# Scores of two graphs in every second slot, score banks doubled, adjacency and values in one bank, two late outputs off VectorE

## What is computed

```python
# per graph; rows are nodes (128), columns features (512)
h = maximum(layernorm(x), 0)
A = adj @ h                                        # layer 0: both weights are adj
x = x + max over columns of maximum(A + b0, 0)     # one number per row
h = maximum(layernorm(x), 0)                       # layer 1
q, k, v = h @ Wq + bq, h @ Wk + bk, h @ Wv + bv
w = softmax(q @ k.T / 8 + (-1e9 where adj == 0))   # per head, over k's nodes
x = x + w @ v
```

## Time and profile before

| | |
|---|---|
| median of three runs | 1332.76 us |
| profiled execution, its own time | 1333.84 us |
| its span, first to last instruction | 1331.8 us |
| TensorE's mean granted clock | 0.993 of full |
| busy share: TensorE, GpSimd, VectorE, ScalarE | 98%, 83%, 81%, 71% |
| longest of the chain that ended last | TensorE, 92% |

### The profile page before, as it was taken

The page is one execution under the profiler, slowest core; times in us unless marked ns, Lnnn a source line. Parts: engine busy times, 40 slices in busy tenths (PEclk is TensorE's granted clock), DMA queues, the critical chain, the costliest instruction groups (busy, mean ns, idle before and its releaser), DMA issues.

```text
span 1331.8 us, 30435 instructions
## 1 busy us (share of the span) xinstructions
PE 1299.0 (98%) x11177; PEld 682.6 (51%) x11177; DVE 1075.3 (81%) x2236; ACT 942.4 (71%) x1423; POOL 1108.3 (83%) x1161
## 2 busy tenths in 40 slices
PE   6999999999999999999999999999999999999994
PEld 3455555555555555555555555555555555555552
DVE  7688887888888888888788788788788878878677
ACT  5977777777777767767767767767777777777652
POOL 4888988888888888888888888889898898898653
PEclk9999999999999999999999999999999999999997
DMA  6355556466565555555556555555565555545334
GB/s 192 72 134 137 126 137 135 122 141 135 120 140 138 120 136 138 123 134 136 128 131 136 131 127 138 134 123 140 135 124 139 135 123 140 130 125 128 88 88 111
DMA packets 437316, 172.19 MB, mean 129 GB/s; under 512 B 402608, under 2 KB 402736, under 8 KB 437168
## 3 DMA queue, kind: packets, MB, share of 16 engines
q1 hardware_dynamic: 435824, 169.98, 54.1%
q10 hardware_dynamic: 1344, 0.27, 0.1%
HBM read 37.03 MB, written 33.55 MB: 53 GB/s over the span
## 4 chain that ended last, share of the span: by engine, by line
PE 92%; DVE 4%; ACT 2%; issue 1%; POOL 0%; DMA 0%; SPq 0%; DVEq 0%; ACTq 0%; POOLq 0%
PE proj L734 49%; PE proj L751 23%; PE sc L770 7%; PE o_ps L785 7%; PE proj L719 6%; DVE y L551 1%; DVE shifted L535 1%; DVE masked L528 1%; DVE row_max L532 1%; ACT qk L387 0%; DMA x_in<-in_x 0%; ACT x L423 0%; ACT qkT L385 0%; ACT h L374 0%; ACT w L428 0%
## 5 line engine op out<-in xcount | busy, mean ns | idle before, releaser
L734 PE MATMUL proj<-hT,w 128*128 128x512 f16 x3072 | 688.2, 380 | 2.4 <-DVE hT L655 2.2
L734 PEld LDWEIGHTS proj<-hT,w 128*128 128x128 f16 x3072 | 290.9, 98 | 350.6 <-issue 5.9
L751 PE MATMUL proj<-w,hT 128*128 128x512 f16 x1536 | 353.5, 380 | 0.0
L385 ACT ACTIVATE qkT<-proj,bqk_up 128x512 f16<-128x512 f32 x256 | 173.4, 677 | 239.7 <-PE proj L734 239.7
L304 POOL TENSOR_TENSOR qkT<-qk,qkT 128x512 f16<-128x512 f32 x256 | 311.7, 1218 | 29.3 <-ACT qk L387 29.1
L311 POOL TENSOR_TENSOR probs<-probs 128x1024 f16<-128x1024 f32 x128 | 273.1, 2133 | 20.3 <-ACT probs L405 20.1
L751 PEld LDWEIGHTS proj<-w,hT 128*128 128x128 f16 x1536 | 150.1, 98 | 181.3 <-issue 1.6
L288 POOL TENSOR_TENSOR h<-h 128x512 f16<-128x512 f32 x126 | 239.1, 1898 | 2.3 <-ACT h L374 1.7
L517 DVE SCALAR_TENSOR_TENSOR v<-proj,v 128x512 f16<-128x512 f32 x128 | 88.5, 691 | 178.7 <-ACT v L393 178.7
L535 DVE TENSOR_TENSOR shifted<-masked,row_max 128x1024 f32<-128x1024 f32 x128 | 213.4, 1667 | 4.4
L551 DVE SCALAR_TENSOR_TENSOR y<-o_ps,out_scale,x 128x64 f32<-128x64 f32 x1024 | 208.3, 277 | 4.5
(11 more groups left out here) (69 smaller groups left out, 1002.7 us busy)
## 6 DMA issues: line engine op xcount, KB each, us to landing
x_in<-in_x SPq DMA_DIRECT2D x128, 256.0 KB, 3.0
out_x<-y SPq DMA_DIRECT2D x128, 256.0 KB, 2.3
probsT<-probs SPq DMA_TRANSPOSE x128, 3.7
hT<-h SPq DMA_TRANSPOSE x124, 3.0
w_raw<-in_L_gnn_Wq SPq DMA_DIRECT2D x4, 256.0 KB, 6.9
w_raw<-in_L_gnn_Wk SPq DMA_DIRECT2D x1, 1024.0 KB, 8.6
w_raw<-in_L_gnn_Wv SPq DMA_DIRECT2D x1, 1024.0 KB, 10.8
bv_rows<-in_L_gnn_bv ACTq DMA_DIRECT2D x1, 256.0 KB, 7.2
```

The lines of the kernel that those rows point to most:

```text
L385: nc.scalar.activation(qk_place(k, u, 0), place, ACT.Identity, scale=P_SCALE, bias=bias).then_inc(qk_head_done, 1)
L734: last = nc.tensor.matmul(proj[:, u % 2, :], w16[:, j, s, c, col * P:(col + 1) * P], hT[:, k // GROUP % HT_GROUPS, t, c, :, :].rearrange(" ...
L751: last = nc.tensor.matmul(v_bank(m), hT[:, m // GROUP % HT_GROUPS, s, c, k % GROUP, :], w16[:, 2, t, c, :], start=(c == 0 and i == 0), sto ...
```

## The change

1. **Scores in pairs.** `sc` has four banks, two for even and two for odd graphs (`score_banks`). TensorE does the scores of graphs k-5 and k-4 one after the other in odd slots, none in even ones. A graph's scores wait for the masked step of the graph two before it. VectorE's `softmax_shift` is split in `softmax_masked` (masked and row maximum) and `softmax_shift` (the subtraction).
2. **Banks given up for it.** Outputs lose their own two banks: the high half takes bank 2, where adjacency was, and the low half bank 1, together with the slot's first chunk (`o_low`, `QK_BANKS`). Adjacency and values share bank 3 (`AV_BANK`). For the shared banks there are new waits: the first chunk for `y_low_done` (four of eight outputs written), outputs' matmuls for `qk_evac`, adjacency for `v_evac`, values for `a_evac`.
3. **Order.** On TensorE adjacency stands between the two chunks, and values come after probabilities times values. On VectorE the adjacency maximum of graph k+2 comes after the subtraction in odd slots, before it in even ones; moments come before the output, which is now that of graph k-6 (`Y_BEHIND` 6). In the first slots the seven first adjacency results lie in banks of `FIRST_BANKS`.
4. **Ending.** `BY_SCALAR` is graphs 123 and 124: VectorE forms their scale vectors, ScalarE writes the eight products (`scaled_out`), GpSimd adds x (`add_x1`). The outputs of graphs 125 and 127 go to score banks (`o_last`).

```diff
 ATTN_BEHIND, OUT_BEHIND, STORE_BEHIND = 5, 6, 7
-V_BEHIND, V_OUT_BEHIND, Y_BEHIND, BV_BEHIND = 5, 6, 7, 4
+V_BEHIND, V_OUT_BEHIND, Y_BEHIND, BV_BEHIND = 5, 6, 6, 4
...
 proj = ps("proj", [P, 4, 512])
-A_BANK, V_BANK = 2, 3
-sc = ps("sc", [P, 2, 512])
-o_ps = ps("o_ps", [P, 2, 512])
-FIRST_BANKS = (proj[:, A_BANK, :], proj[:, V_BANK, :], sc[:, 0, :], sc[:, 1, :], proj[:, A_BANK, :], proj[:, V_BANK, :])
...
-o_view = o_ps[:, :, 0:H // 2 * VW].rearrange("p t (h e) -> p t h e", e=VW)
+O_HIGH, AV_BANK = 2, 3
+sc = ps("sc", [P, 4, 512])
+QK_BANKS = (1, 0)
+o_low = proj[:, 1:O_HIGH + 1, 0:H // 2 * VW].rearrange("p t (h e) -> p t h e", e=VW)
+o_last = sc[:, 0:2, 0:H // 2 * VW].rearrange("p t (h e) -> p t h e", e=VW)
+FIRST_BANKS = (proj[:, AV_BANK, :], sc[:, 0, :], sc[:, 1, :], sc[:, 2, :], sc[:, 3, :], proj[:, AV_BANK, :], sc[:, 0, :])
+FIRST_FREE = (0, 0, 0, 0, 0, 1, 2)
...
+    return FIRST_BANKS[m] if m < len(FIRST_BANKS) else proj[:, AV_BANK, :]
 def v_bank(m):
-    return proj[:, A_BANK if m >= B - V_BEHIND and m % 2 == 0 else V_BANK, :]
+    return proj[:, QK_BANKS[1] if m >= B - V_BEHIND and m % 2 else AV_BANK, :]
+def score_banks(m):
+    return sc[:, 2 * (m % 2):2 * (m % 2) + 2, :]
+def o_view(m):
+    return o_last if m in (B - 3, B - 1) else o_low
...
+    def add_x1(i):
+        m = BY_SCALAR[i]
+        pool.wait_ge(x1_done, m + 1)
+        pool.wait_ge(y_scaled, i + 1)
+        pool.tensor_tensor(y[:, m % Y_RING, :], y[:, m % Y_RING, :], x1[:, m % RING, :], ALU.add).then_inc(y_summed, 1)
+    probs_rest(B, -5)
+    add_bv(B, -4)
+    probs_rest(B, -4)
+    add_bv(B, -3)
+    probs_rest(B, -3)
+    add_bv(B, -2)
+    add_bv(B, -1)
+    add_x1(0)
+    probs_rest(B, -2)
+    add_x1(1)
+    probs_rest(B, -1)
...
+    def scaled_out(i):
+        m = BY_SCALAR[i]
+        act.wait_ge(out_scale_done, m + 1)
+        wait(act, y_stored[m % Y_RING], 16 * (m // Y_RING))
+        for h in range(H):
+            last = nc.scalar.activation(y[:, m % Y_RING, h * HD:h * HD + HD], o_view(m)[:, h // 4, h % 4, 0:HD],
+                                        ACT.Identity, scale=out_scale[:, m % 2, h // 4, h % 4:h % 4 + 1])
+        last.then_inc(y_scaled, 1)
     for k in range(-V_BEHIND, 0):
         v_head(B, k)
         exps(B, k)
+        if k >= -3 and k < -1:
+            scaled_out(k + 3)
...
-    def softmax_shift(base, k, banks=sc):
+    def softmax_masked(base, k):
         if in_range(base, k):
             m = base + k
...
+    def softmax_shift(base, k):
+        if in_range(base, k):
+            m = base + k
             dve.wait_ge(max_done, m + 1)
...
+    def out_scale_of(m):
+        if m >= B - 3:
+            wait(dve, y_scaled, m - B + 4 if m < B - 1 else 2)
+        dve.wait_ge(o_ready, m + 1)
+        nc.vector.tensor_scalar(scaled_sum[:, :, :], o_view(m)[:, :, :, HD], redo[:, 2:3], None,
+                                ALU.mult).then_inc(sum_done, 1)
+        dve.wait_ge(sum_done, m + 1)
+        nc.vector.reciprocal(out_scale[:, m % 2, :, :], scaled_sum[:, :, :]).then_inc(out_scale_done, 1)
     def attention_out(base, k):
...
+            out_scale_of(m)
...
+                if h == H // 2 - 1:
+                    last.then_inc(y_low_done, 1)
             last.then_inc(y_done, 1)
...
     def slot(base, k):
-        if k > 0:
-            adjacency_out(base, k + AMAX_AHEAD)
         v_rest(base, k - V_OUT_BEHIND)
-        softmax_shift(base, k - ATTN_BEHIND)
-        attention_out(base, k - Y_BEHIND)
+        softmax_masked(base, k - ATTN_BEHIND)
+        if k % 2:
+            softmax_shift(base, k - ATTN_BEHIND)
+        if k > ATTN_BEHIND - 2:
+            adjacency_out(base, k + PREP_AHEAD)
+        if k % 2 == 0:
+            softmax_shift(base, k - ATTN_BEHIND)
         if k > 1:
             stats_of(base, k + MOMENTS_AHEAD)
             moments_wait(base, k + MOMENTS_AHEAD)
             moments_of(base, k + MOMENTS_AHEAD)
+        attention_out(base, k - Y_BEHIND)
     for k in range(B):
+        if 0 < k < ATTN_BEHIND:
     v_rest(B, -V_OUT_BEHIND)
-    for i, graph in enumerate(TAIL):
-        softmax_shift(*graph, TAIL_BANKS[i % 2])
-        if i != 2 and i != 4:
-            attention_out(B, i - Y_BEHIND - (i > 2))
-        v_rest(*graph)
+    softmax_masked(B, -5)
+    softmax_shift(B, -5)
+    attention_out(B, -6)
+    v_rest(B, -5)
     for k in range(-4, 0):
+        softmax_masked(B, k)
+        softmax_shift(B, k)
+        v_rest(B, k)
+        if k == -3 or k == -2:
+            out_scale_of(B + k - 2)
+    for k in range(-3, 0):
         attention_out(B, k)
...
         if in_range(base, k):
             pe.wait_ge(h_rest_done, base + k + 1)
-            wait(pe, a_evac, base + k if k > len(FIRST_BANKS) else (0, 0, 0, 0, 1, 2, 5)[k])
+            m = base + k
+            wait(pe, a_evac, FIRST_FREE[m] if m < len(FIRST_FREE) else m)
+            wait(pe, v_evac, m - V_BEHIND - PREP_AHEAD)
...
             wait(pe, qk_evac, 2 * (base + k) - 1 + u % 2)
+            if u % 2 == 0:
+                wait(pe, y_low_done, base + k - Y_BEHIND)
...
             m = base + k
-            wait(pe, v_evac, m if m < B - V_BEHIND + 1 else m - 1)
-            if m == 0:
-                pe.wait_ge(a_evac, len(FIRST_BANKS))
-            if m == B - V_BEHIND + 1:
-                pe.wait_ge(a_evac, B)
+            if m < B - V_BEHIND:
+                wait(pe, v_evac, m)
+            else:
+                pe.wait_ge(v_evac, m - 1)
+                pe.wait_ge(qk_evac, 2 * B)
+            pe.wait_ge(a_evac, min(m + V_BEHIND + PREP_AHEAD + 1, B))
...
-    def scores(base, k, banks=sc):
+    def scores(base, k):
         if in_range(base, k):
             m = base + k
             pe.wait_ge(qk_rest_done, 2 * (m - k % GROUP + GROUP))
-            if banks is sc:
-            if m == 0:
-                pe.wait_ge(a_evac, GROUP)
+            wait(pe, masked_done, m - 1)
+            if m < 2:
+                pe.wait_ge(a_evac, (len(FIRST_BANKS), len(FIRST_BANKS))[m])
...
             pe.wait_ge(probsT_done[k % 2], (m - k % 2) * 8 + 16)
             pe.wait_ge(v_evac, m + 1)
-            wait(pe, y_done, m)
+            wait(pe, qk_evac, min(2 * (m + OUT_BEHIND) + 1, 2 * B))
+            if m < B - 4:
+                wait(pe, y_done, m)
+            elif m == B - 3:
+                pe.wait_ge(masked_done, B - 1)
+            elif m == B - 1:
+                pe.wait_ge(y_done, B - 4)
+            else:
+                pe.wait_ge(y_scaled, 1 if m == B - 4 else 2)
...
     def slot(base, k):
         u = 2 * (k % GROUP)
-        scores(base, k - ATTN_BEHIND)
+        if k % 2:
+            scores(base, k - ATTN_BEHIND)
+            scores(base, k - ATTN_BEHIND + 1)
         qk_chunk(base, k, u)
         if k == 1:
             peak_to_rows(2)
+        adjacency(base, k + PREP_AHEAD)
         qk_chunk(base, k, u + 1)
-        adjacency(base, k + PREP_AHEAD)
         if k == 3:
             peak_to_rows(3)
+        probs_times_v(base, k - OUT_BEHIND)
         v_rows(base, k - V_BEHIND)
-        probs_times_v(base, k - OUT_BEHIND)
     for k in range(B):
         slot(0, k)
-    scores(B, -5)
+    scores(B, -4)
+    scores(B, -3)
     v_rows(B, -5)
-    pe.wait_ge(qk_evac, 2 * B)
-    scores(B, -4, TAIL_BANKS[1])
     v_rows(B, -4)
     probs_times_v(B, -6)
-    pe.wait_ge(masked_done, B - 4)
-    scores(B, -3, TAIL_BANKS[0])
     v_rows(B, -3)
-    pe.wait_ge(masked_done, B - 3)
-    scores(B, -2, TAIL_BANKS[1])
+    scores(B, -2)
     probs_times_v(B, -5)
     v_rows(B, -2)
-    pe.wait_ge(masked_done, B - 2)
-    scores(B, -1, TAIL_BANKS[0])
+    scores(B, -1)
     v_rows(B, -1)
     for k in range(-4, 0):
         probs_times_v(B, k)
```

64 lines of the change are left out of this document (31 added, 33 removed).

## The result

| | before | after |
|---|---|---|
| median of the runs timed side by side | 1333.03 us (4 runs, 1332.33 to 1333.82) | 1323.63 us (4 runs, 1320.26 to 1324.87) |
| profiled execution, its own time | 1333.84 us | 1323.91 us |
| its span | 1331.8 us | 1322.1 us |

A forecast was written before the change was run, and what follows sets the result against it. TensorE, busy 98% of the span, was taken as the bound. Steady part -12.8, start +0.95, scores moved forward +0.65, ending -0.5, late transposes +0.3: -11.4 from 1332.76 gives 1321.4 us, range 1317 to 1330.

The forecast's parts named there:

- The steady part, -12.8: Slots between start and ending: pairing scores saves 0.21 us per pair of slots, 61 times, -12.8 us.
- No new wait in the slots: Steady slots: the new waits on shared banks and the VectorE-ScalarE ring stay hidden, so TensorE does not wait.
- Late transposes, +0.3: Steady slots: the slowest landings of transposed probabilities miss their use by 0.3 us; 0.3 us added in all.
- The ring's room: VectorE and ScalarE wait on each other in a ring: two rounds 19.37 us against 19.86, 0.49 to spare.
- The timetable: Step-by-step times through an odd and an even slot, from which the rooms of the new waits were read.
- The rival that gives 1346: Steady slots: the VectorE-ScalarE ring becomes the bound, 0.9 us more per pair, +13 us in all; chance 0.12.
- The start, +0.95: Up to the steady slots: +1.45 for seven maxima, transposed probabilities 0.15 late, 0.65 lost at 81.87 goes away.
- the 1.45 of a maximum at 54.1: Start: first scores wait for graph 6's maximum, done about 54.1, where they started at 52.69: +1.45 us.
- The ending, 46.0: From the first late scores to the end: 46.0 us against 46.5, -0.5; bounds -3 and +3.5.
- the idle time that the prediction called new: Ending: VectorE idles from 5.4 to 9.7 us after the first late scores, before graph 122's output.
- Sum of the span: Whole span of 1331.8 us: all terms together -11.4, with the ending beginning at 1274.1.

The follow-up runs named there:

- e1: Changed kernel with each graph's scores in a slot of their own again in slots 7 to 126; 1336.72 us, ratio to the kernel before 1.0036.
- e2: Changed kernel with the second graph's scores cut in three passes in odd slots 7 to 125; 1351.63 us, ratio to the kernel before 1.0141.
- e4: Changed kernel with two more 512-column VectorE reductions, result unused, ahead of the subtraction in even slots 8 to 126; 1325.02 us.
- e6: Changed kernel with the adjacency behind the second chunk in slots 0 to 4, as in the kernel before; 1322.99 us.
- e9: Changed kernel with the outputs of graphs 123 and 124 written by VectorE again; 1325.91 us, ratio to the kernel before 0.9948.
- e5: Changed kernel with the first scores waiting for five adjacency maxima in place of seven; 1323.55 us.
- e8: Changed kernel with TensorE doing the values of graph 123 ahead of the scores of 124 and 125 in the ending; 1321.84 us.
- e7: Changed kernel with VectorE doing the output of graph 122 behind the masking and maxima of graph 124 in the ending; 1321.87 us.
- e3: Changed kernel with one more 512-column VectorE reduction, result unused, ahead of the subtraction in even slots 8 to 126; 1323.91 us.
- e12: Changed kernel with new ending orders on VectorE, TensorE and GpSimd, late adjacency in slots 0 to 4, first scores waiting for five maxima; 1320.64 us, ratio 0.9910.

## Why the prediction held, and where it was off

- *The steady part, -12.8.* Right in each figure: 19.85 against 19.86, and slot 8 to slot 126 is 1171.15. e1 and e2 show the cause: a crossing into and out of the 64-row form costs 0.21, whether one is taken away or two are added.
- *No new wait in the slots.* Right. Late transposes, +0.3, did not show: no wait for one before the ending.
- *The ring's room.* The timetable gave 0.49 per pair; the changed kernel had 0.99 and a hold that shrinks with a delay, and two reductions more per pair were absorbed (e4). The rival that gives 1346 was further away than I thought. Two steps failed. A held subtraction was taken as a fixed length; in sum that did no harm to the 0.49, since its two steps took 1.92 and 1.44, 3.36 against twice 1.69, but it hid that a delay costs less than its length. And the 0.50 between 0.49 and 0.99 is small distances that I took too long: values' rest to masked 0.61 twice and not 0.69, masked's maximum to the subtraction with the adjacency maximum between them 1.73 and not 1.26 + 0.67, and one round of ScalarE from exponentials to values' head 3.67 and not 3.76; the rest is 0.05.
- *The start, +0.95.* Mis-sized. First, the wait itself: 2.04 and not the 1.45 of a maximum at 54.1. I counted the seventh maximum but not what moving the adjacency between the chunks does to ScalarE's queue: 0.63 by e6. Then small waits of 0.25 and 0.17 at 67.92 and 71.32. The measured start is 1.35 later than forecast at slot 8, and 0.4 of it (slot 4 at 47.17 and not 46.76) is no effect of the change: TensorE's slow first stretch was that much longer in this execution, and in e1 and e9, with the same program up to there and a first chunk at 20.05 and 20.03, slot 4 began at 46.82 and 46.86.
- *The ending, 46.0.* Right in sum (46.2), and the idle time that the prediction called new is there, 4.54 where 4.3 was forecast. In its parts two errors cancel, so the good sum is in part luck: the last subtraction ends 30.8 after the first late scores, not 31.9, ScalarE's eight products take 1.73 (at 1298.58) and not 2; behind it 15.4 pass, not 14.0, because the last graph's rest stands behind GpSimd's addition and behind a rest that took 3.10. Missed outright: 0.72 before the first late scores, for GpSimd's rest of q and k that stands behind a rest of probabilities in its queue.
- *Sum of the span:* forecast -11.4. The first late scores came at 1275.94, not at 1274.1, +1.8 (start 1.35, the missed wait 0.7, 0.2 back in the slots), the ending +0.2, the transposes -0.3: -9.7, as measured.
- The other parts of the change (double score banks, shared bank, order) cost 3.6 us by e1, in the start and the ending. They are the price of the pairing, and e5 to e8 show that some of it is order alone.

## To carry to other kernels

Count crossings between matmul forms as instructions with a price read from distances of starts, and put work of one form together: 0.21 us in 20 was 1% of this kernel. Before moving one engine's instruction, follow what else waits in every queue it passes, SyncE's too: the reorder that looked like 1.2 us of gain cost 2.5. And do not take from TensorE's idle row what an edit will gain: at the start 2.04 us of it were worth 0.3 by e5, while in the ending VectorE's idle time was worth nearly all (2.7 less idle gave 2.6 in e7, 2.1 less gave 2.0 in e8).

## What was unexpected

**TensorE's slow stretches move.** The first chunk takes 2.75 us in one execution and up to 5.28 in others. In the second of these its 12 matmuls take 5.07 until the next group starts (20.04 to 25.11), 0.42 each, where the steady part has 0.216: half the pace, that of the level of 1.2 in place of 2.4 GHz. In e3 and in the changed kernel:

```profile
18.85 2.75 PE L816 MATMUL proj<-hT,w 128*128 128x512 f16 x12 [2.03 <-DVE hT L718]
```

```profile
20.04 5.28 PE L810 MATMUL proj<-hT,w 128*128 128x512 f16 x12 [2.20 <-DVE hT L716]
```

The granted clock reads 1.00 for 20 to 25 us in the second, so here the pace tells it and the record does not. The Trainium skill (TensorE: Matmul & The Clock Gate, Part 1: The HAM clock gate) says that the number of slow matmuls at the start differs between runs of one kernel. The traces agree, as far as kernels with the same program up to there can show it: the first chunk takes 2.75 in e3, 4.01 in e4, 5.01 in e8 and 5.28 in e9. After the wait of 2.04 for the maxima a second such stretch follows in eight of the ten profiles that have this wait, but not in the changed kernel's own or in e4's: in e9 the next chunk takes 4.25 where it takes 2.76, with a granted clock of 0.66 for 55 to 60 us, and slot 4 to slot 8 lasts 39.40 in place of 38.18 (beside such an execution e5's 37.86 is 1.5 less, not 0.3):

```profile
54.89 1.67 PE L840 MATMUL sc<-qkT 64*128 64x128 f16 x48 [2.04 <-DVE a_max L556]
56.49 4.25 PE L804 MATMUL proj<-hT,w 128*128 128x512 f16 x12
```

None follows in e5, e6 and e12, with a wait of 1.42 or none. But in e5 and e6 two values groups of the ending took 6.35 and 6.45 (5.35 in the changed kernel), and the ending 51.3; between 1276 and 1284 the granted clock is 0.79 in e5 and 1.00 in the changed kernel. That may be why their medians hardly fell. The same groups are slow in e1 and e4. The changed kernel has a slow stretch in its ending too, but later: the values group at 1287.60 takes 4.02 (granted clock 0.70 from 1287 to 1292). It costs nothing to the end, since in e3, where that group takes 2.76, the ending is as long. These pieces (2.5 in the first chunk, 1.2 behind the wait, 1.6 in the ending) are as large as the spread of 4.6 us between runs; that they are its whole cause was not shown, since only one execution of each kernel has a profile.
